# A ternary-weight feed-forward with attention: signs of four weight halves made by ScalarE, the sum of the down weight moved forward, and the high rows of the second chunk copied by GpSimd

## What is computed

```python
def ternary_quant(w):                       # scale = mean(|w|) over the whole matrix
    scale = jnp.mean(jnp.abs(w)) + EPS
    return jnp.clip(jnp.round(w / scale), -1.0, 1.0) * scale
def _L0_ffn_ref(x, W_up, W_gate, W_down):   # up, gate: 256 -> 1024, down: 1024 -> 256
    up   = jnp.einsum('bsd,ed->bse', x, wu)
    gate = jnp.einsum('bsd,ed->bse', x, wg)
    return jnp.einsum('bse,de->bsd', jax.nn.silu(up) * gate, wd)
x = L0_attn_x                               # (16, 256, 256) f32
x = x + 0.5 * _L0_ffn_ref(_layernorm(x), W_up, W_gate, W_down)
x = x + _L0_attn_ref(_layernorm(x), Wq, bq, Wk, bk, Wv, bv)    # 16 heads, 4 groups, causal
x = x + 0.5 * _L0_ffn_ref(_layernorm(x), W_up, W_gate, W_down)
```

## Time and profile before

| | |
|---|---|
| median of 3 runs | 603.82 us (603.62 to 603.99) |
| the profiled execution | 604.03 us, of which the trace spans 602.3 us |
| TensorE matmul busy | 566.0 us, 94% |
| VectorE busy | 485.8 us, 81% |
| ScalarE busy | 412.1 us, 68% |
| GpSimd busy | 176.7 us, 29% |
| granted TensorE clock, mean | 1.0 of full |

### The profile page before, as it was taken

One profiled execution on the slowest core, in us unless ns is written; L12 is line 12 of the kernel. 1 busy time (PEld: TensorE's weight loads), 2 busy tenths in 40 slices (PEclk: granted clock), 3 DMA queues, 4 the chain that ended last, 5 costly groups with the idle time before them and its releaser, 6 DMA issues.

```text
span 602.3 us, 12457 instructions
## 1 busy us (share of the span) xinstructions
PE 566.0 (94%) x4276; PEld 344.9 (57%) x4276; DVE 485.8 (81%) x1865; ACT 412.1 (68%) x775; POOL 176.7 (29%) x229
## 2 busy tenths in 40 slices
PE   2869999999999989999999999998999999999998
PEld 2336556655666755656566656554445666656666
DVE  6998988889875889888988897888597687756654
ACT  4637756765655378898888888887767656765742
POOL 3015201101530035555545455667501101101100
PEclk9999999999999999999999999999999999999999
DMA  8701001100205151414141424231201111211112
GB/s 313 219 19 35 19 19 36 35 19 19 36 17 125 37 111 56 92 54 93 56 90 58 95 62 92 77 59 30 45 1 36 53 54 36 70 54 53 36 35 71
DMA packets 71679, 37.90 MB, mean 63 GB/s; under 512 B 33984, under 2 KB 71104, under 8 KB 71616
## 3 DMA queue, kind: packets, MB, share of 16 engines
q1 hardware_dynamic: 71616, 37.11, 24.3%
HBM read 18.22 MB, written 10.49 MB: 48 GB/s over the span
## 4 chain that ended last, share of the span: by engine, by line
PE 79%; DVE 10%; ACT 6%; issue 2%; POOL 2%; DMA 1%; DVEq 0%; POOLq 0%; ACTq 0%
PE bank L1112 33%; PE bank L1124 17%; PE bank L1211 7%; PE bank L1279 5%; PE bank L1270 5%; PE bank L1238 5%; ACT shared L566 3%; PE bank L1293 2%; PE bank L1284 2%; DVE sm_out L951 2%; PE bank L1103 1%; DVE hid L814 1%; DVE hl L829 1%; PE bank L1249 1%; POOL xn L395 1%
## 5 line engine op out<-in xcount | busy, mean ns | idle before, releaser
L951 DVE CUSTOM_DVE_ANT_0 sm_out<-bank,mask 128x256 f16<-128x256 f32 (+1 forms) x512 | 153.6, 352 | 25.7 <-PE bank L1238 23.4
L456 ACT ACTIVATE silu<-bank,w_scale 128x512 f32<-128x512 f32 x128 | 87.3, 683 | 117.0 <-PE bank L1112 116.1
L814 DVE SCALAR_TENSOR_TENSOR hid<-silu,h_unit,bank 128x512 f32<-128x512 f32 x128 | 95.0, 742 | 62.5 <-ACT silu L456 62.1
L566 ACT ACTIVATE shared<-bank,qk_scale 128x512 f32<-128x512 f32 x192 | 121.5, 681 | 21.7 <-PE bank L1270 20.8
L1124 PE MATMUL bank<-wT_down,hh 128*128 128x256 f16 x512 | 118.2, 273 | 1.8 <-DVE hl L829 1.6
L1124 PE MATMUL bank<-wT_down,hl 128*128 128x256 f16 x512 | 118.2, 273 | 0.0
L1112 PE MATMUL bank<-xh,wT_gate 128*128 128x512 f16 x256 | 97.1, 379 | 4.4 <-DVE hid L814 4.4
L1112 PE MATMUL bank<-xh,wT_up 128*128 128x512 f16 x256 | 98.0, 383 | 1.2 <-DVE xl L758 1.2
L829 DVE TENSOR_TENSOR hl<-hid,hh 128x512 f16<-128x512 f32 x128 | 98.1, 767 | 0.0
L1112 PE MATMUL bank<-xl,wT_up 128*128 128x512 f16 x256 | 98.0, 383 | 0.0
L404 POOL TENSOR_TENSOR xnl<-xn,xnh 128x1024 f16<-128x1024 f32 x13 | 27.7, 2134 | 238.1 <-ACT xn L493 180.4
(11 more groups left out here) (115 smaller groups left out, 750.3 us busy)
## 6 DMA issues: line engine op xcount, KB each, us to landing
q_st<-q_scratch SPq DMA_DIRECT2D x32, 256.0 KB
q_scratch<-q_hl SPq DMA_DIRECT2D x16, 256.0 KB, 2.2
out_dram<-x SPq DMA_DIRECT2D x7, 512.0 KB, 2.9
x<-in_x_dram SPq DMA_DIRECT2D x1, 3072.0 KB, 15.6
k_scratch<-k_hl SPq DMA_DIRECT2D x16, 128.0 KB, 2.4
k_st<-k_scratch SPq DMA_DIRECT2D x16, 128.0 KB
x<-in_x_dram SPq DMA_DIRECT2D x2, 512.0 KB, 4.6
shared<-in_w_up_t_dram SPq DMA_DIRECT2D x2, 512.0 KB, 6.2
```

The lines of the kernel that those rows point to most:

```text
L456: act.activation(silu[:, e % 2, :], U[e % 2][:, :], ACT.Silu, scale=w_scale[:, 0:1]).then_inc(silu_ready, 1)
L566: act.activation(prob[:, place % 2, i, :], score_bank(n, i)[:, :], ACT.Exp, scale=qk_scale[:, 4:5]).then_inc(exp_done, 1)
L814: dve.scalar_tensor_tensor(out=hid[:, e % 4, :], in0=silu[:, e % 2, :], scalar=h_unit[:, 0:1], in1=GT[e % 2][:, :], op0=ALU.mult, op1=ALU. ...
L951: ins = dve.tensor_tensor_reduce(sm_out[:, i, cols], SM[i][:, cols], mask[:, S - size:S], 1.0, MASKED, ALU.add, ALU.max, rowmax[:, seq_par ...
```

## The change

In neutral words: ScalarE computes `Sign(raw + threshold)` in fp16 (`sign_of`) for the second half of up, the second half of gate and both halves of down; VectorE then makes each of these with one operation, `(raw > threshold) min sign`. ScalarE's two `abs_sum` of down stand before chunk 0 instead of beside its pieces 0 and 1; TensorE's `weight_sum(2)` stands between the first two up groups and the first gate group instead of after piece 2; `scale_of(2)` and the two `y_scale` steps stand beside piece 0 instead of piece 3; the two ternary operations of down beside pieces 5 and 7 instead of 4 and 5. Chunk 1's `xn` is made beside pieces 1 and 2 instead of 2 and 3, and its `xnh` is a GpSimd copy of `xn` instead of VectorE's own computation. The statistics of chunk 2 are taken in piece 6 of chunk 0 and piece 0 of chunk 1 (before: pieces 6 and 7 of chunk 0), its `rstd` steps in pieces 1 and 2 of chunk 1 (before: piece 0), and its `xnh` and `xn` by ScalarE in pieces 3 and 4 (before: 2 and 3).

```diff
@@ -106,7 +106,7 @@
 
 
         w_abs = hh[:, 1, 0:4, :].rearrange("p e n -> p (e n)")
-        w_neg = [hl[:, 1, 2 * i:2 * i + 2, :] for i in range(4)]
+        w_sign = w_neg = [hl[:, 1, 2 * i:2 * i + 2, :] for i in range(4)]
 
         xT = sb("xT", [P, ND, TC])
         q_hl = sb("q_hl", [P, 2, 2, TC], F16)
@@ -143,6 +143,7 @@
         dve_self = sem("dve_self")
         tern_ready = sem("tern_ready")
         thr_ready = sem("thr_ready")
+        sign_ready = sem("sign_ready")
         most_ready = sem("most_ready")
         bound_ready = sem("bound_ready")
         attn_w_ready = sem("attn_w_ready")
@@ -403,6 +404,8 @@
                 pool.wait_ge(xl_ready, 16 * n)
                 pool.tensor_tensor(xnl[:, :, :], xn[:, :, :], xnh[:, :, :], ALU.subtract).then_inc(xnl_ready, 1)
 
+            pool.wait_ge(xn_ready, 2)
+            pool.tensor_copy(xnh[:, :, :], xn[:, :, :]).then_inc(xnh_ready, 1)
             low_part(1, 1)
             step(pool.memset(val[:, :, :, :, :], 0.0))
             pool.memset(val[:, :, :, :, DH:DH + 1], 1.0).then_inc(const_ready, 1)
@@ -440,6 +443,16 @@
                 act.activation(w_abs[:, 0:F], w_raw[:, m, half * F:(half + 1) * F], ACT.Abs,
                                accum_out=w_sum[:, m, half:half + 1]).then_inc(abs_ready, 1)
 
+            def sign_of(m, half):
+
+                act.wait_ge(thr_ready, m + 1)
+                if m == 2:
+                    act.wait_ge(tern_ready, half + 1)
+                    raw, sign = w_raw[:, 2, half * F:(half + 1) * F], w_sign[half].rearrange("p e n -> p (e n)")
+                else:
+                    raw, sign = half_of(w_raw[:, m, :], half), w_sign[2 * half + m]
+                act.activation(sign, raw, ACT.Sign, bias=w_thr[:, m, 0:1]).then_inc(sign_ready, 1)
+
             def first_x_high(d):
 
                 act.wait_ge(tr_ready, d + 1)
@@ -464,15 +477,17 @@
 
                 def first_chunk(e):
 
-                    if e < 2:
-                        abs_sum(2, e)
-                    if e in (2, 3):
+                    if e == 0:
+                        sign_of(1, 1)
+                    if e in (1, 2):
                         act.wait_ge(shift_ready, 1)
-                        for t in range(2 * e - 4, 2 * e - 2):
+                        for t in range(2 * e - 2, 2 * e):
                             ins = act.activation(xn[:, t, :], x[:, TT + t, :], ACT.Identity,
                                                  scale=rstd[:, 0, TT + t:TT + t + 1], bias=shift[:, 0, TT + t:TT + t + 1])
-                        if e == 3:
+                        if e == 2:
                             ins.then_inc(xn_ready, 1)
+                    if e in (3, 4):
+                        sign_of(2, e - 3)
 
                 def next_normed(c, begin):
 
@@ -514,7 +529,7 @@
 
                 chunk(0, 0, None if ph else first_chunk)
                 for i in range(NC // 2 - 1):
-                    chunk(2 * i + 1, 1, next_normed(2 * i + 2, 2))
+                    chunk(2 * i + 1, 1, next_normed(2 * i + 2, 2 if ph or i else 3))
                     chunk(2 * i + 2, 0, next_normed(2 * i + 3, 2))
                 chunk(NC - 1, 1, None if ph else attention_start)
                 hidden_high(64 * ph + 63, 1, NE - 1)
@@ -643,6 +658,9 @@
                     abs_sum(m, half)
             for d in range(ND):
                 first_x_high(d)
+            sign_of(0, 1)
+            for half in range(2):
+                abs_sum(2, half)
             feed_forward(0)
             attention()
             feed_forward(1)
@@ -670,18 +688,21 @@
 
                 cols = slice(half * F // 2, (half + 1) * F // 2)
                 raw, neg = half_of(w_raw[:, m, :], half), w_neg[2 * half + m]
-                step(dve.tensor_scalar(neg, raw, w_thr[:, m, 1:2], None, ALU.is_lt))
+                if half:
+                    dve.wait_ge(sign_ready, m + 1)
+                else:
+                    step(dve.tensor_scalar(neg, raw, w_thr[:, m, 1:2], None, ALU.is_lt))
                 dve.scalar_tensor_tensor(out=(wT_up, wT_gate)[m][:, :, cols], in0=raw, scalar=w_thr[:, m, 0:1],
-                                         in1=neg, op0=ALU.is_gt, op1=ALU.subtract).then_inc(tern_ready, 1)
+                                         in1=neg, op0=ALU.is_gt,
+                                         op1=ALU.min if half else ALU.subtract).then_inc(tern_ready, 1)
 
             def ternary_down(half):
 
-                raw, neg = w_raw[:, 2, half * F:(half + 1) * F], w_neg[2 + half].rearrange("p e n -> p (e n)")
-                dve.wait_ge(tern_ready, 4)
-                step(dve.tensor_scalar(neg, raw, w_thr[:, 2, 1:2], None, ALU.is_lt))
+                raw, sign = w_raw[:, 2, half * F:(half + 1) * F], w_sign[half].rearrange("p e n -> p (e n)")
+                dve.wait_ge(sign_ready, half + 3)
                 dve.scalar_tensor_tensor(out=wT_down[:, half * 4:half * 4 + 4, :].rearrange("p e n -> p (e n)"), in0=raw,
-                                         scalar=w_thr[:, 2, 0:1], in1=neg, op0=ALU.is_gt,
-                                         op1=ALU.subtract).then_inc(tern_ready, 1)
+                                         scalar=w_thr[:, 2, 0:1], in1=sign, op0=ALU.is_gt,
+                                         op1=ALU.min).then_inc(tern_ready, 1)
 
             counted = {"stats": 0, "moments": 0}
 
@@ -789,13 +810,13 @@
                         for n, at, begin in ((2, 2, 0), (3, 4, 0), (4, 4, 4), (5, 5, 0), (6, 6, 6)):
                             if c == at:
                                 rstd_in(n, begin)
-                        if c == 0 and e > 5:
+                        if (c, e) in ((0, 6), (1, 0)):
                             dve.wait_ge(ld_xr, 16)
-                            ln_stats_of(2, range(2 * e - 12, 2 * e - 10))
-                        if c == 0 and e == 7:
+                            ln_stats_of(2, range(0, 2) if e else range(2, 4))
+                        if c == 1 and e == 0:
                             ln_moments(2)
-                        if c == 1 and e == 0:
-                            ln_rstd_steps(1, range(RSTD_STEPS))
+                        if c == 1 and e in (1, 2):
+                            ln_rstd_steps(1, range(6 * e - 6, 6 * e))
                         for q, at, begin in ((3, 1, 4), (4, 1, 6), (NC, 2, 2), (5, 2, 6), (NC + 1, 3, 2),
                                              (6, 3, 6), (NC + 2, 4, 2), (7, 4, 6), (NC + 3, 5, 6), (NC + 4, 6, 4),
                                              (NC + 5, 7, 0)):
@@ -841,17 +862,11 @@
 
                     if e == 0:
                         ternary(1, 1)
-                    if e == 1:
-                        for t in range(TT):
-                            ins = dve.tensor_scalar(xnh[:, t, :], x[:, TT + t, :], mv[:, 0, TT + t, 0:1],
-                                                    rstd[:, 0, TT + t:TT + t + 1], ALU.subtract, ALU.mult)
-                        ins.then_inc(xnh_ready, 1)
-                    if e == 3:
                         scale_of(2)
                         step(dve.tensor_tensor(y_scale[:, 0:1], w_scale[:, 0:1], w_scale[:, 1:2], ALU.mult))
                         step(dve.tensor_tensor(y_scale[:, 1:2], y_scale[:, 0:1], w_scale[:, 2:3], ALU.mult))
-                    if e in (4, 5):
-                        ternary_down(e - 4)
+                    if e in (5, 7):
+                        ternary_down(e // 2 - 2)
 
                 def next_norm(e):
 
@@ -1142,8 +1157,8 @@
                                 pe.wait_ge(tern_ready, 1 + gate)
                                 up_or_gate(0, 0, par, gate)
                                 up_or_gate(1, 1, par, gate)
-                        if ph == 0 and first and e == 2:
-                            weight_sum(2)
+                                if gate == 0:
+                                    weight_sum(2)
                         if down:
                             if e < 2:
                                 pe.wait_ge(hl_ready, s - 4 + 3 * e)
```

## The result

The changed kernel takes 600.92 us (median of four runs, 600.48 to 601.5) against 603.9: the ratio is 0.9949, with a 95% interval of 0.9937 to 0.9962. It is faster, by 3.0 us; the forecast was 600.3 in a range of 599.0 to 602.9. The profiled execution takes 600.96 us, and its trace spans 599.2.

The account below looks back on a forecast made before the run. VectorE was taken to bound the end of chunk 0 and start of chunk 1, TensorE what follows. 4.1 - 0.3 (lock) - 0.3 (chunk 2) = 3.5 us gained: 600.3 us, range 599.0 to 602.9.

Parts of the forecast that it names:

- the landmark: TensorE's start of the second half of chunk 1's first down tile; claimed at 39.45 instead of 43.54 us.
- the walk: Priced engine lists through chunk 0's pieces: hid 0 at 21.25, last hl ending at 39.4, a 4.1 us gain.
- the lock: GpSimd's SBUF reads and VectorE's two-SBUF-input operations hold each other up; cost at hl 2 taken as 0.3 us.
- rival D: No change: ScalarE has less room, 2.5 to 4 us of further waits in pieces 2 to 6; 603.8, chance 0.07.
- The unknown prices: Rows not in the trace: ScalarE's Sign on 128x1024 taken as 1.05 us, GpSimd's fp16 copy as 1.2.
- Rival C: Sign is outside silu's table: eight table loads, 10.3 us on ScalarE before the attention; 608.0, chance 0.07.
- A: Rival: GpSimd's copy takes 5.5, chunk 1's rows late; 601.7, chance 0.11. As measure: hid 0 to the landmark.
- Chunk 2, 0.3: Shift done 6.5 after the landmark, low rows at 16.7 where TensorE wants 16.5: a stall taken as 0.3 us.
- B: Rival: chunk 2 takes back more, stall 1.5; 601.9, chance 0.12. As measure: the landmark to chunk 2's second down half.
- C: As measure, not rival: time from chunk 2's second down half to the end of the span.

Follow-up runs that it names:

- e2: Changed kernel, but VectorE computes chunk 1's high rows beside piece 1 again and GpSimd's copy is gone: 602.38 us.
- e7: Changed kernel with GpSimd's copy done twice before chunk 1's low rows: 601.97 us.
- e4: Changed kernel with chunk 2's 12 rstd steps at once in piece 0 of chunk 1, its xnh and xn in pieces 2 and 3: 601.83 us.
- e9: Changed kernel with chunk 2's statistics and moments in piece 3 of chunk 0, rstd at once, rows in pieces 2 and 3: 600.07 us.
- e0: The changed kernel run again, without edits, as reference point: 601.02 us, 0.9951 of the kernel before.
- e8: Changed kernel with TensorE's weight_sum(2) behind the two gate groups of piece 0 instead of in front: 600.89 us.
- e1: Changed kernel, but VectorE makes all four weight halves with two operations again and ScalarE makes no signs: 602.92 us.

## Why the prediction was right

**The mechanism held.** VectorE's list to the last `hl` of chunk 0 was the bound, ScalarE's list took its place in pieces 3 to 5, and VectorE ran without a wait from `hid` 5 on. From `hid` 0 to the landmark the walk had 39.45 - 21.25 = 18.2; the profiles show 18.3. Silu held `hid` for 1.6 us in three waits. The chain's numbers give about 2.1; the 0.4 by which the lock lengthened `hl` 3 stands in front of the third wait and makes up most of the difference.

So rival D, more waits for ScalarE than the walk had, did not come.

**The unknown prices were near.** Sign 1.14 for 1.05: two of them lie on the path, 0.18 in all. GpSimd's copy 1.04 for 1.2. Chunk 1's low rows landed at 30.32 + 2.8 = 33.1 for 33.3. Rival C died at once, since no table load was added (Sign runs on the load that silu has); so did A, the copy being a fifth of its price.

**The lock, 0.3, was taken and not paid.** `hl` 2 kept its 0.69 and GpSimd waited for it; `hl` 3 was held to 1.09, and `hid` 5 waited for silu anyway. e2 and e7 show the other side, 1.18 and 0.41, by when the two engines' instructions meet. The Trainium skill's rule ("SBUF — State Buffer", "SBUF: two separate sides": the one that starts first has the ports for its whole instruction) agrees with these rows, in both directions: `hl` 1 of e2, which started second, took 2.24 behind the subtraction, and the changed kernel's subtraction 2.69 beside `hl` 2, where the two starts are 0.01 apart and don't show who was first.

**Chunk 2, 0.3, was mis-sized: 0.71.** The shift came 6.2 after the landmark for 6.5, and chunk 2's start was 0.23 late. What I hadn't seen is the second wait, 0.48 in front of the second down half: "TensorE wants them 16.5 after it" stops at the start of chunk 2, while VectorE's list stays full to the last `hl` of chunk 1. The change moved 1.08 us of statistics and moments across the landmark. I had counted them in the lateness of the shift, and not in VectorE's list behind it. e4 (22.18) and e9 (21.01), which differ in this alone for B, show it: they differ by 1.17. The changed kernel pays 0.71 of it, because the split and the later pieces win 0.49 (e4).

**And 0.35 wasn't a term at all.** One matmul in the attention waits for a transfer in some executions (C 538.1) and not in others (537.7), in experiments too, whatever was edited. So it isn't a fixed cost of the change: the first profile of the changed kernel has it, e0 doesn't, and it went against the changed kernel in the profile that was compared. It is in seven of the twelve profiles with the change (0.11 to 0.49 us) and in neither of the two without; whether the earlier start of the attention makes it more frequent isn't shown.

With what was measured: 4.16 less 0.71 is 3.45, where I had 3.5. The central estimate was nearly right with two errors of opposite sign (the lock 0.3 too dear, chunk 2 0.4 too cheap); the medians say 3.0 and 3.1. In the first profile the rest is the 0.35, in e0's it is `hid` 0, 0.47 later than in the kernel before. Being so close is luck; what the runs bear out is the walk to the landmark. Of the rivals, B had the right place, and under half its price (0.7 for 1.5).

**What each part is worth**, each undone alone: by A, signs 1.90, copy on GpSimd 1.18, early sums 0.67 (by the medians 1.90, 1.36 and 0.35). They sum to 3.75 of 4.06, but the gain in A has a fourth part: the statistics and moments that left it, 1.07 us of VectorE's list before the change (41.09 to 42.16 in its trace, with the landmark at 43.54). This is work moved and not saved, and B shows what it costs behind. No run puts it back alone, so how the four share the 4.06 stays open.

## What to carry to other kernels

Walk the lists of both engines to the first point that the bound engine waits for, and then once more from there to the next such point: work that is moved behind the first is paid at the second (0.71 here), and e9 shows that its right place is under a wait that exists anyway. Where two engines exclude each other from a port, the order in which their instructions meet can cost more than their durations (in e2 a lock of 1.55 for operations of 1.30); operations of one SBUF input that stand where the engine waits anyway were nearly free (in e9, 1.74 us of them). Compare profiles from the last common event instead of from the start of the span; here that brought differences from a scatter of 1.7 us down to 0.03.

## What the hardware showed that I had not expected

**When the matmuls become fast.** The first 512-column matmuls stand 0.43 us apart, later ones 0.215, a ratio of two as between the clock's two levels of 1.2 and 2.4 GHz, although the granted clock reads 1.00 for this stretch. The first fast one came at 18.99 to 22.28 us in fourteen profiles, although the first up matmul started at 16.21 to 16.62 in all of them. In e8:

```profile
20.00 0.63 PE L1127 MATMUL bank<-xl,wT_gate 128*128 128x512 f16 x1
20.43 0.59 PE L1127 MATMUL bank<-xh,wT_gate 128*128 128x512 f16 x1
20.85 0.38 PE L1127 MATMUL bank<-xl,wT_gate 128*128 128x512 f16 x1
21.07 0.38 PE L1127 MATMUL bank<-xh,wT_gate 128*128 128x512 f16 x1
```

The changed kernel waits for the first gate group with `hid` 0, so this moves its end; its runs scatter over 1.9 us in e0 (600.25 to 602.19), those of the kernel before beside it over 0.9 (603.84 to 604.73), where VectorE isn't ready before 21.1 in any case. That the wider scatter comes from this fits `hid` 0 in the profiles (21.08 and 21.67 for the changed kernel, 21.20 and 21.11 for the one before); it isn't shown for each run.

**A long wait can cost the clock.** In e1's profile TensorE was busy for only 0.36 us in 40 to 42, and then:

```profile
40.00:42.00 2.00, 0.36 (x2) 0.00 (x0) 2.00 (x3) 0.36 (x2) 0.00 (x0) 1.00 0.00 0
42.00:44.00 2.00, 1.52 (x8) 1.09 (x9) 1.97 (x8) 0.48 (x1) 0.00 (x0) 0.62 0.03 8
44.00:46.00 2.00, 2.00 (x7) 0.82 (x6) 1.83 (x9) 0.00 (x0) 0.00 (x0) 0.53 0.00 0
46.00:48.00 2.00, 2.00 (x15) 1.27 (x13) 1.19 (x3) 1.20 (x2) 0.00 (x0) 1.00 0.00 0
```

The granted clock fell to 0.62 and 0.53, near the lower level, for some 3 us, after a wait of 2.12 us for `hl` (to 42.48). This made B 22.72 there (21.7 in its neighbours). Of e1's eleven runs exactly the three slowest (604.6 to 604.75; the others 602.4 to 603.31) have a mean granted clock of 0.997 instead of 1.0, and the profiled one is among them; so, if the wait is alike in all eleven, it doesn't cost the clock each time. The trace says what TensorE did before the fall, not more. In the changed kernel the wait at this place is 1.33, and no profile of it shows a fall.
